# Adding the causal mask in PSUM with VectorE instead of with a bf16 matmul

## The chip, the cores and the metric

One NeuronCore of a Trainium2 chip runs the whole program in one launch. The metric is device time in microseconds (us); for the kernel before it is the median of three runs, 2414.44 us (2411.25 to 2418.63).

## What is computed

One transformer layer on x of shape (1, 2048, 512): causal attention with grouped key heads, a residual and a layer norm, then a mixture of experts (64 experts, top 8, capacity 256) with a residual and a layer norm. The change touches the attention only:

```python
# H, HKV, HD = 16, 4, 128; G = H // HKV = 4; T = 2048; q and k after RoPE
scores = jnp.einsum('bgjtd,bjsd->bgjts', q, k) * scale
mask = jnp.tril(jnp.ones((T, T), dtype=bool))
scores = jnp.where(mask[None, None, None], scores, -jnp.inf)
wei = jax.nn.softmax(scores, axis=-1)
out = jnp.einsum('bgjts,bjsd->bgjtd', wei, v)
```

## The kernel before

The program has five stages, one after the other: projections with RoPE, attention (`stage_attend`, lines 421 to 798), output projection and routing, experts, and the combination. Each stage writes out the instruction stream of every engine by hand, with semaphores between them.

The attention stage loops over the four key heads j. A head has U = 64 steps, one for each block of 128 query rows (16 of them) and each of the four query heads of the group. Step u works on query block u // 4. I count blocks from 1: block b holds the steps 4(b−1) to 4b−1, and its score rows are 128·b columns wide, because nothing to the right of the diagonal tile is computed. Up to 1024 columns (block 8) a step has one score group; from block 9 on it has two, one of 1024 columns and one with the rest. The only tile that needs a mask is the last one of a row, 128x128 on the diagonal. PSUM holds two score buffers of 1024 columns, `S[:, 0]` and `S[:, 1]`: narrow steps take them in turns, wide steps use one for each group. There are two buffers for transposes (`TP`) and two for outputs (`O`).

All matmuls on scores and values are three fp32r products of high and low parts (`split3`). In iteration i the engines do:

- TensorE (lines 583 to 664): the scores of step i (L603) and at their end the mask, a bf16 matmul of the identity with the mask tile that accumulates on the diagonal tile (L605). It waits for `exped`, with which ScalarE frees the score buffer. Then come the transposes of the probabilities of step i−3 (L615) and a half of the weighing with V for a pair of steps, five steps back (L634). Wide steps go: scores of group 0, two sets of transposes, scores of group 1, weigh, other transposes.
- VectorE (lines 712 to 784): in odd iterations the low part of an output (L760), after ScalarE's high part; then the row maximum of the first group (L732), the reciprocal of step i−1 (L743, or L745 and L748), the low parts of the first two sets of transposes (L754), the maximum of the second group and the combined maximum (L732, L736), and the low parts of the other transposes. Its queue is in this order, whatever is ready first.
- ScalarE (lines 666 to 710): in odd iterations the high part of an output (L696), high parts of transposes (L690), then exp of a group with the row sum (L681; L678 for the factor between groups), which frees the score buffer.
- GpSimd (L795) multiplies the probabilities by the reciprocal of the sum before they are transposed. SyncE loads K, V and Q and stores the outputs.

The mask tile and the identity come by DMA (`const_in`); ScalarE casts both to bf16 (L669, L670), and TensorE waits for the two casts at its start (`const_ready`, L663). The mask tile holds 0 and −1e30. The semaphore `scored` is incremented by the last matmul of a group, which is the mask matmul for the last group of a step.

Of the kernel before, what the change touches and what calls it, by code (L numbers as in the profile page):

```python
# [22 lines left out]
BF16 = mybir.dt.bfloat16  # L23
I32 = mybir.dt.int32
U32 = mybir.dt.uint32
ALU = mybir.AluOpType
# [3 lines left out]
P = 128  # L30
# [32 lines left out]
def split3(a, b):  # L63

    return ((a[LO], b[HI]), (a[HI], b[LO]), (a[HI], b[HI]))
# [355 lines left out]
def stage_attend(nc, passed, ident_d, mask_d, qk_d, v_d, o_d, wo, wo_raw, wo_in):  # L421

    U = NB * G
    blk = lambda u: u // G
    width = lambda u: (blk(u) + 1) * P
    ngrp = lambda u: 1 if width(u) <= 1024 else 2
# [12 lines left out]
    def score_group(u, a):  # L439

        return (u % 2) if ngrp(u) == 1 else a

    before, last_use = {}, {}
    for u in [u - U for u in range(U)] + list(range(U)):
        for a in range(ngrp(u % U)):
            s = score_group(u % U, a)
# [3 lines left out]
    with ExitStack() as ctx:  # L450
        def sb(name, shape, dt=F32):
            return ctx.enter_context(nc.sbuf_tensor("p2_" + name, shape, dt))

        def ps(name, shape):
            return ctx.enter_context(nc.psum_tensor("p2_" + name, shape, F32))

        def sem(name):
            return ctx.enter_context(nc.semaphore("p2_" + name))

        ident = sb("ident", [P, P])  # L460
        identb = sb("identb", [P, P], BF16)
        maskb = sb("maskb", [P, P], BF16)
        maskf = sb("maskf", [P, P])
        kT = sb("kT", [P, NT, 2, 512], F32R)
        v = sb("v", [P, NB, 2, HD], F32R)
# [13 lines left out]
        S = ps("S", [P, 2, 1024])  # L479
        TP = [ps(f"TP{k}", [P, 4, P]) for k in range(2)]  # L480
        O = [ps(f"O{k}", [P, 2, P]) for k in range(2)]

        const_in, const_ready = sem("const_in"), sem("const_ready")
        next_in, k_first, v_first, v_free = sem("next_in"), sem("k_first"), sem("v_first"), sem("v_free")
        k_in = [None] + [sem(f"k_in{c}") for c in range(1, NT)]
        v_in = [None] + [sem(f"v_in{c}") for c in range(1, NT)]
# [30 lines left out]
        def lagged(i, lag, first):  # L517

            u = i - lag
            return (u, 0) if u >= 0 else None if first else (u + U, 1)  # L520


        def steps(eng, step, tail):
            def body(j, first):
                for i in range(U):
                    step(j, i, first)
            loop(eng, HKV, body)
            for i in range(U, U + tail + 1):
                step(HKV - 1, i, False)
# [53 lines left out]
        @block.tensor  # L583
        def _(pe):
            def scores(j, u, a, first):
                b, g, tc = blk(u), u % G, u // 16
                if u == 0:
                    pe.wait_ge(k_first, j + 1)
                elif u % 16 == 0 and a == 0:
                    pe.wait_ge(k_in[tc], j * 16 + 16)  # L590
                if first and u < G - 1:
                    pe.wait_ge(q_first[u], 16)
                if a == 0 and u % 16 == (G - 1 if first and tc == 0 else 0):
                    pe.wait_ge(q_in[tc % 2], j * 32 + (16 + 16 * (tc // 2)))
                qs = [q[tc % 2][:, g, s, (b % 4) * P:(b % 4 + 1) * P] for s in (HI, LO)]
                if not (first and before[(u, a)] < 0):
                    pe.wait_ge(exped, j * SG[U] + (before[(u, a)] + 1))
                s = score_group(u, a)
                for c0 in range(a * 1024, min(width(u), a * 1024 + 1024), 512):
                    w = min(512, width(u) - c0)  # L600
                    out = S[:, s, c0 - a * 1024:c0 - a * 1024 + w]
                    for n, (x, y) in enumerate(split3(qs, [kT[:, c0 // 512, s2, 0:w] for s2 in (HI, LO)])):
                        mm = nc.tensor.matmul(out, x, y, start=(n == 0), stop=(n == 2))  # L603
                    if c0 + w == width(u):
                        mm = nc.tensor.matmul(S[:, s, width(u) - P - a * 1024:width(u) - a * 1024], identb[:],  # L605
                                              maskb[:], start=False, stop=True, skip_group_check=True)
                mm.then_inc(scored, 1)

            def turn(j, back, u, t):
                if t % 2 == 0:  # L610
                    pe.wait_ge(normed, j * SG[U] + (SG[u] + t // 2 + 1 - back * SG[U]))
                n = TG[u] + t
                pe.wait_ge(turn_lo, j * TG[U] + (n + 1 - back * TG[U]))
                for s in range(4 * t, min(4 * t + 4, blk(u) + 1)):
                    mm = nc.tensor.transpose(TP[n % 2][:, s % 4, :], prob[u % KEEP][:, s * P:(s + 1) * P], ident[:])  # L615
                mm.then_inc(turned, 1)

            def weigh(j, back, p, part, half=None):

                nb = blk(2 * p) + 1  # L620
                cut = (nb + 1) // 2
                lo, hi = ((0, cut), (cut, nb))[part]
                mid = {None: hi, 0: (lo + hi) // 2, 1: (lo + hi) // 2}[half]
                if part == 0 and half != 1:
                    if p == 0:
                        pe.wait_ge(v_first, j + 1)
                    elif p % 8 == 0:
                        pe.wait_ge(v_in[p // 8], j * 16 + 16)
                    pe.wait_ge(turn_lo, j * TG[U] + (TG[2 * p + 2] + FREE - back * TG[U]))
                    pe.wait_ge(o_lo, j * PAIRS + (p + 1 - back * PAIRS))  # L630
                for s in range(mid, hi) if half == 1 else range(lo, mid):
                    for n, (x, y) in enumerate(split3([v[:, s, h, :] for h in (HI, LO)],
                                                      [pT[p % 2][h][:, s, :, :] for h in (HI, LO)])):
                        mm = nc.tensor.matmul(O[p % 2][:], x, y, start=(s == 0 and n == 0),  # L634
                                              stop=(s == nb - 1 and n == 2))
                        if s == nb - 1 and n == 2:
                            mm.then_inc(weighed, 1)
                        elif p == PAIRS - 1 and s == cut - 1 and n == 2:
                            mm.then_inc(v_free, 1)

            def step(j, i, first):
                at = lagged(i, LAG, first)
                turns = [(j, at[1], at[0], t) for t in range(ntr(at[0]))] if at and i < U + LAG else []
                at = lagged(i, WEIGH, first)
                halves = [None]
                if len(turns) > 2 and (i >= U or ngrp(i) == 1):
                    halves = [0, 1]
                if i < U and len(halves) == 1:
                    scores(j, i, 0, first)
                if len(halves) == 2:  # L650
                    weigh(j, at[1], at[0] // 2, at[0] % 2, 0)
                for args in turns[0:2]:
                    turn(*args)
                if i < U and len(halves) == 2:
                    scores(j, i, 0, first)
                if i < U and ngrp(i) == 2:
                    scores(j, i, 1, first)
                if at and i < U + WEIGH:
                    weigh(j, at[1], at[0] // 2, at[0] % 2, halves[-1])
                for args in turns[2:]:  # L660
                    turn(*args)

            pe.wait_ge(const_ready, 2)  # L663
            steps(pe, step, WEIGH - 1)

        @block.scalar
        def _(act):
            act.wait_ge(const_in, 32)
            nc.scalar.copy(identb[:], ident[:]).then_inc(const_ready, 1)  # L669
            nc.scalar.copy(maskb[:], maskf[:]).then_inc(const_ready, 1)  # L670
            act.sem_inc(weighed, FREE)

            def exp(j, u, a):
# [37 lines left out]

        @block.vector
        def _(dve):
            dve.sem_inc(turn_lo, FREE)
            dve.sem_inc(o_lo, FREE)

# [10 lines left out]
            def row_max(j, u, a):  # L727
                k, wide = u % KEEP, ngrp(u) == 2
                dve.wait_ge(scored, j * SG[U] + (SG[u] + a + 1))
                w = min(1024, width(u) - a * 1024)  # L730
                out = (nmax if a == 0 else nmax1) if wide else nm
                r = nc.vector.reduce_max(out[:, k:k + 1], S[:, score_group(u, a), 0:w], AX_X, negate=True)  # L732
                r.then_inc(max_part if a == 1 else max_ready, 1)
                if a == 1:
                    dve.wait_ge(max_part, j * (SG[U] - U) + (SG[u + 1] - u - 1))
                    nc.vector.tensor_tensor(nm[:, k:k + 1], nmax[:, k:k + 1], nmax1[:, k:k + 1], ALU.min  # L736
                                            ).then_inc(max_ready, 1)
# [958 lines left out]
```

## Time and profile before

| | |
|---|---|
| Median of three runs | 2414.44 us (2411.25 to 2418.63) |
| Profiled execution, first to last instruction | 2450.7 us |
| Difference of the profiled span to the median | 36.3 us, 1.5% |
| Attention stage in it | about 328 to 1395 us |
| Mean granted clock of TensorE | 0.934 of full speed |
| TensorE busy / weight loads / VectorE / ScalarE / GpSimd | 2104.8 / 1802.7 / 1749.9 / 1371.8 / 1125.8 us |

Of the profiled execution only the span is given, with no separate time around it; all durations below are from this one execution. TensorE is called PE in the rows, its weight loads PEld, VectorE DVE, ScalarE ACT and GpSimd POOL. Matmuls are pipelined, and a matmul's duration is its latency: what it costs a stream is read from the distance of starts. Where an engine's idle time is shown, the name behind the arrow is what ended it.

### The profile page before, as it was taken

The numbers are of one execution on the slowest core, as the hardware profiler recorded it, in microseconds if no ns is written. First come the engines' busy times: TensorE is split into PE (matmuls) and PEld (weight loads), VectorE is DVE, ScalarE is ACT, GpSimd is POOL, SyncE is SP. The second block draws the span as 40 slices with busy tenths as digits, with TensorE's granted clock in tenths as the row PEclk, the third lists the DMA queues.
The fourth block names the chain that finished last, engine by engine and source line by source line (L and its number), as shares of the span: only waits on it lengthen the run. The fifth ranks groups of instructions, "written<-read, shape, count | busy, mean of one in ns | idle before, by whom it ended". The sixth has DMA issues, their size and how long they took to land. (4 is left out here: it accounts for less than half of the span.)

```text
span 2450.7 us, 43821 instructions
## 1 busy us (share of the span) xinstructions
PE 2104.8 (86%) x13313; PEld 1802.7 (74%) x13313; DVE 1749.9 (71%) x3146; ACT 1371.8 (56%) x2755; POOL 1125.8 (46%) x1093
## 2 busy tenths in 40 slices
PE   8999969999999999999999989982999999996000
PEld 6777758988899888988899877772888888884000
DVE  5899967876787677776787645553777777774657
ACT  3899946665676567665676532222566666663000
POOL 1455523332333223332333226664666666664675
PEclk9999979999999999999999999995999999997555
DMA  7444462012411051104300065432788888884775
GB/s 241 176 193 193 188 250 88 27 57 86 135 62 57 24 190 70 57 22 162 121 35 23 23 237 174 174 128 97 255 263 278 263 265 273 265 268 160 216 235 182
DMA packets 145296, 380.61 MB, mean 155 GB/s; under 512 B 19584, under 2 KB 37120, under 8 KB 140544
## 3 DMA queue, kind: packets, MB, share of 16 engines
q1 hardware_dynamic: 120576, 311.61, 37.1%
q0 software_dynamic: 24576, 67.20, 8.3%
q8 instruction: 75, 1.23, 0.2%
q14 instruction: 69, 0.57, 0.1%
HBM read 252.78 MB, written 125.96 MB: 155 GB/s over the span
## 5 line engine op out<-in xcount | busy, mean ns | idle before, releaser
L603 PE MATMUL p_S<-p_kT,p_q 128*128 128x512 f32 (+3 forms) x1920 | 475.0, 377 | 31.8 <-DMA p_q<-qk_scratch 25.1
L603 PEld LDWEIGHTS p_S<-p_kT,p_q 128*128 128x128 f32 x1920 | 324.7, 190 | 81.0 <-issue 27.3
L795 POOL TENSOR_SCALAR p_prob<-p_prob,p_inv,p_part 128x1024 f32<-128x1024 f32 x128 | 153.0, 1196 | 496.1 <-DVE p_inv L748 496.1
L615 PE MATMUL p_TP<-p_ident,p_prob 128*128 128x128 f32 x2176 | 303.5, 274 | 1.8 <-DVE p_pT1l L754 1.8
L795 POOL TENSOR_SCALAR p_prob<-p_prob,p_inv 128x128 f32<-128x128 f32 (+7 forms) x256 | 191.5, 748 | 241.4 <-DVE p_inv L743 241.4
L732 DVE TENSOR_REDUCE p_nmax<-p_S 128x1 f32<-128x1024 f32 (+7 forms) x256 | 251.7, 983 | 23.1 <-PE p_S L603 22.1
L615 PEld LDWEIGHTS p_TP<-p_ident,p_prob 128*128 128x128 f32 x2176 | 245.5, 141 | 25.9 <-DVE p_pT1l L754 5.6
L690 ACT CAST p_pT1h<-p_TP 128x512 fp32r<-128x512 f32 (+3 forms) x320 | 154.8, 526 | 153.5 <-PE p_TP L615 153.3
L690 ACT CAST p_pT0h<-p_TP 128x512 fp32r<-128x512 f32 (+3 forms) x320 | 155.1, 527 | 150.4 <-PE p_TP L615 149.2
L634 PE MATMUL p_O<-p_pT0h,p_v 128*128 128x256 f32 x1088 | 227.6, 293 | 6.0 <-DVE p_pT0l L754 6.0
L634 PE MATMUL p_O<-p_pT1h,p_v 128*128 128x256 f32 x1088 | 226.0, 292 | 5.6 <-issue 3.2
L754 DVE TENSOR_TENSOR p_pT1l<-p_TP,p_pT1h 128x512 fp32r<-128x512 f32 (+3 forms) x320 | 182.3, 603 | 60.2 <-ACT p_pT1h L690 59.4
L754 DVE TENSOR_TENSOR p_pT0l<-p_TP,p_pT0h 128x512 fp32r<-128x512 f32 (+3 forms) x320 | 182.2, 603 | 50.1 <-ACT p_pT0h L690 49.1
L681 ACT ACTIVATE p_prob<-p_S,p_nm 128x128 f32<-128x128 f32 (+7 forms) x256 | 189.6, 741 | 28.7 <-DVE p_nm L732 27.3
L416 POOL TENSOR_TENSOR p_qr<-p_rc,p_rs 128x512 f32<-128x512 f32 x80 | 131.4, 1643 | 120.6 <-DVE p_rs L365 120.6
L634 PEld LDWEIGHTS p_O<-p_pT0h,p_v 128*128 128x128 f32 x1088 | 178.7, 191 | 7.0 <-issue 5.1
L634 PEld LDWEIGHTS p_O<-p_pT1h,p_v 128*128 128x128 f32 x1088 | 178.0, 191 | 7.0 <-issue 3.6
L916 PE MATMUL p_acc<-p_woh,p_ot 128*128 128x512 f32 x512 | 174.6, 413 | 8.4 <-DMA p_ot<-o_scratch 8.4
L1104 POOL DMA_INDIRECT slot_scratch<-p_tok,p_slot_i x128 | 127.0, 992 | 93.3 <-DVE p_slot_i L1065 55.5
L1550 POOL DMA_INDIRECT p_rows<-y_scratch,p_idx x128 | 135.2, 1056 | 65.1 <-issue 35.9
L1466 POOL DMA_INDIRECT p_xg<-x_scratch,p_idx x128 | 129.3, 1010 | 73.3 <-POOL p_idx L1462 52.0
L681 ACT ACTIVATE p_prob<-p_S,p_nmax 128x1024 f32<-128x1024 f32 x128 | 144.2, 1127 | 24.2 <-DVE p_nmax L732 22.8
(212 smaller groups left out, 5061.0 us busy)
## 6 DMA issues: line engine op xcount, KB each, us to landing
p_w_raw<-in_gu SPq DMA_DIRECT2D x64, 768.0 KB
qk_scratch<-p_qout SPq DMA_DIRECT2D x80, 512.0 KB, 2.6
o_scratch<-p_oT SPq DMA_DIRECT2D x128, 256.0 KB, 2.1
p_ot<-o_scratch SPq DMA_DIRECT2D x32, 1024.0 KB
y_scratch<-p_y SPq DMA_DIRECT2D x128, 256.0 KB
p_q<-qk_scratch SPq DMA_DIRECT2D x15, 2048.0 KB, 9.2
p_w_raw<-in_gu SPq DMA_DIRECT2D x64, 256.0 KB
v_scratch<-p_vout SPq DMA_DIRECT2D x16, 512.0 KB, 3.2
```

Source lines behind the costliest of these rows:

```text
L416: nc.gpsimd.tensor_tensor(qr[t][:], rc[t % 2][:], rs[t % 2][:], ALU.add).then_inc(q_rot, 1)
L603: mm = nc.tensor.matmul(out, x, y, start=(n == 0), stop=(n == 2))
L615: mm = nc.tensor.transpose(TP[n % 2][:, s % 4, :], prob[u % KEEP][:, s * P:(s + 1) * P], ident[:])
L634: mm = nc.tensor.matmul(O[p % 2][:], x, y, start=(s == 0 and n == 0), stop=(s == nb - 1 and n == 2))
L681: nc.scalar.activation(prob[k][:, a * 1024:a * 1024 + w], S[:, score_group(u, a), 0:w], ACT.Exp, bias=top[:, k:k + 1], accum_out=rsum[:, k ...
L690: nc.scalar.copy(pT[p % 2][HI][:, 4 * t:4 * t + m, u % 2, :], TP[n % 2][:, 0:m, :]).then_inc(turn_hi, 1)
L732: r = nc.vector.reduce_max(out[:, k:k + 1], S[:, score_group(u, a), 0:w], AX_X, negate=True)
L754: nc.vector.tensor_tensor(pT[p % 2][LO][:, 4 * t:4 * t + m, u % 2, :], TP[n % 2][:, 0:m, :], pT[p % 2][HI][:, 4 * t:4 * t + m, u % 2, :].b ...
L795: nc.gpsimd.tensor_scalar(prob[k][:, cols], prob[k][:, cols], inv[:, k:k + 1], scale, ALU.mult, ALU.mult).then_inc(normed, 1)
L916: mm = nc.tensor.matmul(acc[k][:], a, w, start=(n == 0 and m == 0), stop=(n == H - 1 and m == 2))
L1466: nc.gpsimd.indirect_dma_start(out=xg[k][c][:], out_offset=None, in_=x1_d, in_offset=bass.IndirectOffsetOnAxis(ap=idx[k][:, c:c + 1], axis ...
L1550: nc.gpsimd.indirect_dma_start(out=rows[k][n][:], out_offset=None, in_=y_d, in_offset=bass.IndirectOffsetOnAxis(ap=idx[k][:, n:n + 1], axi ...
```

## The change

The mask matmul, the two bf16 tiles and the casts go. TensorE waits for the DMA of the constants instead of for the casts. In the last score group of every step VectorE adds the fp32 mask tile to the diagonal tile in PSUM, waits for its own addition, and then takes the row maximum. `scored` is now incremented by the last matmul of the scores.

```diff
@@ stage_attend @@
-        identb = sb("identb", [P, P], BF16)
-        maskb = sb("maskb", [P, P], BF16)
...
-        const_in, const_ready = sem("const_in"), sem("const_ready")
+        const_in, covered = sem("const_in"), sem("covered")
...
                         mm = nc.tensor.matmul(out, x, y, start=(n == 0), stop=(n == 2))
-                    if c0 + w == width(u):
-                        mm = nc.tensor.matmul(S[:, s, width(u) - P - a * 1024:width(u) - a * 1024], identb[:],
-                                              maskb[:], start=False, stop=True, skip_group_check=True)
                 mm.then_inc(scored, 1)
...
-            pe.wait_ge(const_ready, 2)
+            pe.wait_ge(const_in, 32)
             steps(pe, step, WEIGH - 1)
 
         @block.scalar
         def _(act):
-            act.wait_ge(const_in, 32)
-            nc.scalar.copy(identb[:], ident[:]).then_inc(const_ready, 1)
-            nc.scalar.copy(maskb[:], maskf[:]).then_inc(const_ready, 1)
             act.sem_inc(weighed, FREE)
...
         @block.vector
         def _(dve):
+            dve.wait_ge(const_in, 32)
             dve.sem_inc(turn_lo, FREE)
...
                 out = (nmax if a == 0 else nmax1) if wide else nm
+                if a == ngrp(u) - 1:
+                    last = S[:, score_group(u, a), w - P:w]
+                    nc.vector.tensor_tensor(last, last, maskf[:], ALU.add).then_inc(covered, 1)
+                    dve.wait_ge(covered, j * U + u + 1)
                 r = nc.vector.reduce_max(out[:, k:k + 1], S[:, score_group(u, a), 0:w], AX_X, negate=True)
```

## Rows read from the trace of the kernel before

**Rows 1.** The page's head and its line of busy times

```profile
span 2450.7 us, 43821 instructions
...
PE 2104.8 (86%) x13313; PEld 1802.7 (74%) x13313; DVE 1749.9 (71%) x3146; ACT 1371.8 (56%) x2755; POOL 1125.8 (46%) x1093
```

**Rows 2.** Busy time by stretch, third head: blocks 1-2, 3-4, 6-10, 11-16

```profile
core 0: us, PE busy (x) PEld busy (x) DVE busy (x) ACT busy (x) POOL busy (x), PEclk, DMA share, GB/s
851.50:877.70 26.20, 23.44 (x194) 22.04 (x192) 13.98 (x39) 11.68 (x34) 4.75 (x9) 1.00 0.39 137
877.70:890.30 12.60, 12.19 (x86) 9.95 (x85) 10.37 (x30) 10.24 (x30) 5.29 (x9) 1.00 0.67 214
898.90:971.20 72.30, 71.95 (x515) 64.67 (x514) 56.29 (x119) 50.26 (x119) 24.14 (x27) 1.00 0.32 111
971.20:1121.70 150.50, 147.91 (x1052) 133.16 (x1051) 113.63 (x219) 98.56 (x219) 47.99 (x48) 1.00 0.10 36
```

**Rows 3.** Groups by line and shape: busy us, mean ns, idle before

```profile
L605 PE MATMUL p_S<-p_maskb,p_identb 128*128 128x128 bf16 x256 | 59.6, 233 | 0.0
...
L754 DVE TENSOR_TENSOR p_pT1l<-p_TP,p_pT1h 128x128 fp32r<-128x128 f32 x32 | 9.0, 280 | 0.0
```

**Rows 4.** Timeline of TensorE: mask ahead of transposes, mask ahead of a weigh (start, us)

```profile
928.20 0.23 PE L605 MATMUL p_S<-p_maskb,p_identb 128*128 128x128 bf16 x1
928.26 0.61 PE L615 MATMUL p_TP<-p_ident,p_prob 128*128 128x128 f32 x4
...
1340.17 0.23 PE L605 MATMUL p_S<-p_maskb,p_identb 128*128 128x128 bf16 x1
...
1340.41 0.28 PE L634 MATMUL p_O<-p_pT0l,p_v 128*128 128x256 f32 x1
1340.53 0.28 PE L634 MATMUL p_O<-p_pT0h,p_v 128*128 128x256 f32 x1
```

**Rows 5.** Timeline of ScalarE: its first exp of the stage

```profile
329.82 0.37 ACT L681 ACTIVATE p_prob<-p_S,p_nm 128x128 f32<-128x128 f32 x1 [8.57 <-DVE p_nm L732]
```

**Rows 6.** Timeline, two steps of block 4 (u = 13, 14, then 15)

```profile
885.45 0.68 DVE L732 TENSOR_REDUCE p_nm<-p_S 128x1 f32<-128x512 f32 x1
...
886.58 0.68 DVE L732 TENSOR_REDUCE p_nm<-p_S 128x1 f32<-128x512 f32 x1
...
887.97 0.36 ACT L696 CAST p_oT<-p_O 128x256 fp32r<-128x256 f32 x1
888.37 0.42 DVE L760 TENSOR_TENSOR p_oT<-p_O,p_oT 128x256 fp32r<-128x256 f32 x1 [0.40 <-ACT p_oT L696]
...
888.71 0.68 DVE L732 TENSOR_REDUCE p_nm<-p_S 128x1 f32<-128x512 f32 x1
```

**Rows 7.** Timeline of VectorE: row maxima of even steps, blocks 5, 6 and 7

```profile
890.28 0.82 DVE L732 TENSOR_REDUCE p_nm<-p_S 128x1 f32<-128x640 f32 x1 [0.24 <-PE p_S L605]
...
898.93 0.96 DVE L732 TENSOR_REDUCE p_nm<-p_S 128x1 f32<-128x768 f32 x1 [0.43 <-PE p_S L605]
...
904.06 0.96 DVE L732 TENSOR_REDUCE p_nm<-p_S 128x1 f32<-128x768 f32 x1 [0.60 <-PE p_S L605]
...
915.16 1.09 DVE L732 TENSOR_REDUCE p_nm<-p_S 128x1 f32<-128x896 f32 x1 [0.69 <-PE p_S L605]
```

**Rows 8.** Timeline, from block 9's last step (u = 35) to block 10

```profile
948.49 0.42 DVE L760 TENSOR_TENSOR p_oT<-p_O,p_oT 128x256 fp32r<-128x256 f32 x1 [0.97 <-ACT p_oT L696]
948.83 1.21 DVE L732 TENSOR_REDUCE p_nmax<-p_S 128x1 f32<-128x1024 f32 x1
...
951.10 0.19 ACT L681 ACTIVATION_READ_ACCUMULATOR p_prob<-p_S,p_nmax 128x1 f32 x1
...
951.34 1.68 PE L603 MATMUL p_S<-p_kT,p_q 128*128 128x512 f32 x6
```

**Rows 9.** Timeline of block 16 (u = 61, then the scores of 62)

```profile
1099.47 1.22 DVE L732 TENSOR_REDUCE p_nmax<-p_S 128x1 f32<-128x1024 f32 x1
...
1100.72 0.16 DVE L736 TENSOR_TENSOR p_nm<-p_nmax 128x1 f32<-128x1 f32 x1
...
1102.19 0.30 ACT L678 ACTIVATE p_part<-p_nmax,p_nm 128x1 f32<-128x1 f32 x1
...
1103.64 1.66 PE L603 MATMUL p_S<-p_kT,p_q 128*128 128x512 f32 x6
```

## The prediction

> **What bounds the kernel now.** I read the head and the busy line of the page first [rows 1]: TensorE is busy for 86% of the span and VectorE for 71%. Such shares average stages with different limits, so the second view is the busy time in stretches of the attention stage. The stage does the same work for each of four key heads; I use the third, from 850.8 to 1121.7 us [rows 2]. A head has 64 steps (u = 0 to 63); four steps make a block, and in block b the score rows are 128·b columns wide. The reader is to see two regimes. From 898.9 us on (block 6) TensorE has almost no gap (71.95 of 72.30, 147.91 of 150.50) and VectorE is busy for 78 and 76%. In blocks 3 and 4, 877.7 to 890.3, VectorE and ScalarE are each at 82 and 81%, and TensorE, at 97%, hides short waits behind its modelled ends. The granted clock is 1.00 in all of them. So the change trades time on an engine that is the limit in the wide blocks for time on one that is nearly the limit in the narrow ones, and the question is where each amount counts. The answer is the same in each head, so what a block gives counts 16 times (4 steps, 4 heads).
>
> **Removed: 256 mask matmuls on TensorE.** The group shows x256 at 233 ns [rows 3], but that is latency. What one takes from the stream is read from starts [rows 4]. Ahead of a weigh, from the mask matmul's start to the start of the second weigh matmul pass 1340.41 − 1340.17 = 0.24 us, where two weigh matmuls are otherwise 0.12 apart (1340.41 to 1340.53): 0.24 − 0.12 = **0.12 us**. That is the case of the 32 wide steps of a head (blocks 9 to 16). Ahead of transposes, as in nearly all narrow steps, the first starts 0.06 after the mask matmul and four take (0.61 − 0.27)/3 = 0.11 each, which is their usual pitch: **0.07 us**. If TensorE were the limit everywhere this were 128 × 0.12 + 128 × 0.07 = 24 us.
> The Trainium skill (TensorE: Matmul & The Clock Gate, section Back-to-back issue gap) gives about 81 ns for one weight load and matmul of 128 columns in a stream. By that figure 256 would be worth 21 us, and the wide steps 0.08 instead of 0.12 each; the trace's larger number is used.
>
> **Removed: two casts on ScalarE** ahead of the stage. Nothing: ScalarE waits 8.57 us after them for the first row maximum [rows 5]. If that wait were gone they would be worth at most 0.7 us (two 128x128 instructions, each no longer than the 0.37 of the exp in that row).
>
> **Added: 256 VectorE additions of a 128x128 tile in PSUM, and a wait of VectorE on its own result.** No row shows VectorE writing PSUM. The nearest is the 128x128 subtraction that reads PSUM, 280 ns [rows 3]. Bounds: a 128x1 instruction takes 0.16 [rows 9], the 128x256 subtraction from PSUM 0.42 [rows 8]. I take 0.28. The dependent instruction after a VectorE result starts 0.03 later (a maximum ends at 1099.47 + 1.22 = 1100.69, the next starts at 1100.72 [rows 9]). So **0.31 us** a step, 0.19 to 0.45 by the bounds. Queued behind it on VectorE are the row maximum, the reciprocal that releases GpSimd, and the low parts that release the transposes' PSUM; behind the maximum ScalarE's exp, which frees the score buffer.
> The Trainium skill (VectorE: DVE Perf Modes, section Rules for kernel authors) says that chained VectorE instructions each pay the pipeline and that the op count is to be kept small. It speaks against this change; its formula for an fp32 two-tensor op would give 0.29 for 128 elements, an estimate from that page, which would leave the sum as it is within 1 us.
>
> **Where the 0.31 counts, block by block.**
> Blocks 3 and 4. The limit is a round trip over two steps [rows 6]: maximum of the odd step at 885.45, maximum of the even step at 886.58, then its exp on ScalarE, then the output cast on ScalarE (887.97), for which VectorE idles 0.40, the low part of the output (888.37), and the next odd maximum at 888.71. These 3.26 us are VectorE and ScalarE one after the other, and TensorE is not in them. Both additions of the two steps lie in it; the idle time of 0.40 is no room, since what it waits for is behind the even addition. +0.31 a step; TensorE's saving is worth nothing.
> Blocks 5 to 8. The same round trip, but the even maximum now waits for TensorE [rows 7]: 0.24 in the first pair of block 5 and nothing that the view prints in the second (I take 0.19 for both), 0.43 and 0.60 in block 6, 0.69 in block 7 and more in block 8. Independent VectorE instructions overlap by 0.08 (888.37 + 0.42 against 888.71 [rows 6]), so the room is the wait plus 0.08. Block 5: (0.62 − 0.27)/2 = +0.18 a step. Block 6: (0.62 − 0.60)/2 = +0.01. Blocks 7 and 8: room for both, TensorE sets the pace, −0.07.
> Blocks 9 and 10. The mask lies in the second of two score groups, but the round trip over two steps passes through it once: low part of the output (948.49), odd first maximum (948.83, behind it), exp, whose buffer TensorE waits for (scores again at 951.34) [rows 8], even maximum, and then the even second group with its addition. In this pair nothing is free: the scores follow the exp at once. Wider groups leave some room, so I allow 0.1 as a mean of the two blocks: (0.31 − 0.10)/2 = +0.11 a step; TensorE's saving is lost here too. Block 11 lies between this and the next case, 0.
> Blocks 12 to 16. The addition is hidden: in block 16 the combined maximum is there at 1100.88, and ScalarE, behind the high parts of the last transposes, takes it at 1102.19 [rows 9]. If that cover of 1.3 us were gone, each would cost 0.31. The time to 1103.64, where TensorE reuses the buffer, runs through the weigh and the transposes after the mask, so the saving counts whole: −0.12 a step.
> Blocks 1 and 2. VectorE is busy for 14 of 26.9 us [rows 2], mostly waiting for the end of the head before. The first step and the last already wait for VectorE, the others gain 0.07: +1 us in all, −2 to +10 by the same prices in none or in all 32 steps.
>
> **The sum.** Per step 0.31 + 0.31 + 0.18 + 0.01 − 0.07 − 0.07 + 0.11 + 0.11 + 0 − 5 × 0.12 = +0.29; times 16 is 4.6, with blocks 1 and 2 **+5.6 us**. The profiled execution spans 2450.7 us, so it would span 2456.3. It was 36 us (1.5%) longer than the median of the runs, 2414.4; I put the difference on the median: **2420 us**. With 0.19 for the addition the blocks give −0.35 a step, −5.6 us; with 0.45 it reaches block 7 and 11, +1.21 a step, 19.4 and 2 more. So this case goes from 2409 to 2436, most of it 2412 to 2429. A measurement of this kernel tells about 0.3% (7 us) from no change.
>
> **Rivals.**
> *The VectorE round trip binds further than block 6.* Slower. Mechanism: PSUM writes cost VectorE more than reads, or the low parts, which come 0.62 late in even steps, hold the transposes. It decides once the two additions exceed the room of 0.69 + 0.08 = 0.77 in block 7, that is at 0.39 each. Then blocks 3 to 7 pay 0.31 or more (80 × 0.31 = 25), blocks 9 to 11 0.16 (8), and blocks 8 and 12 to 16 give back 11: +22 us, **2436**. For: no row shows such a write, and in block 6 the room is just used up. Against: the nearest rows are 0.28 and TensorE has almost no gap in the stretch from 898.9 [rows 2]. 0.22.
> *Part of the addition is hidden.* Faster. Mechanism: the 0.40 idle ahead of the output's low part takes one of two additions, and the free parts of blocks 9 to 11 are larger. Blocks 3 and 4 then give +0.16, 5 to 7 −0.07, 8 the same, 9 to 11 −0.12: 0.32 − 0.28 − 0.36 − 0.60 = −0.92 a step, −15 us, **2400**. Against it: ScalarE's cast starts right behind the even exp in [rows 6]. 0.17.
> *TensorE's clock falls.* TensorE waits for longer in blocks 3 and 4 with fewer matmuls. At 1.2 GHz their 12.19 us of matmuls would take up to 24; some of it fills the waits, so I take +9 us a head over my forecast, **2456**. Against: the clock stayed at 1.00 (2.4 GHz) through blocks 1 and 2, where TensorE has 2.8 us of gaps [rows 2]. 0.03. The Trainium skill (TensorE: Matmul & The Clock Gate, section Why this matters for your kernels) warns of clock drops after idle gaps; no gap of this stage brought one on.
> *It doesn't do what it says:* the mask matmuls were hidden under weight loads, and nothing comes back. The 0.24 in [rows 4] speaks against it. Without the 0.12 and 0.07 of blocks 7, 8 and 12 to 16 the sum is +17 us, 2431: inside the first rival's reach and counted there.
>
> **Chances.** My forecast 0.58: 0.38 within 0.3%, 0.20 above it. Round trip 0.22 and clock 0.03, all slower. Hidden 0.17: 0.13 faster, 0.04 within. Faster 0.13, same 0.42, slower 0.45. Range 2403 to 2437: it takes in the bounds of the addition and most of the faster case; forecast and slower cases hold most of the chance on one side.
>
> **What would show it.** In the changed profile: additions of 0.26 to 0.32 us; step pairs of blocks 3 and 4 longer by 0.6 us (3.26 to 3.9); blocks 12 to 15 shorter by 0.12 a step with TensorE still without gaps; weigh matmuls at 0.12 right behind the scores; blocks 7 and 8 slightly shorter. I am wrong if the addition takes over 0.4, if blocks 3 and 4 hardly grow, if blocks 12 to 16 don't shrink, or if the time moves outside the attention stage.

## The result, and the profile after

The changed kernel takes 2419.61 us (median of six runs, 2416.75 to 2424.07), the kernel before 2414.27 us (six runs on the same chip). The ratio of the runs is 1.0026, with a 95% interval of 1.0014 to 1.0038: slower by 0.26%, inside what I had called hard to tell from no change, and 0.4 us beside the predicted 2420. In microseconds the ratio says +6.3 (3.4 to 9.2), the two medians alone +5.3. Differences of timed runs below are worked out from the ratio.

The span of the changed kernel's profiled execution can't be set against the 2450.7 us of [rows 1]. To judge by the stages behind the attention (last section), the kernel before was profiled on a slower chip, of the kind on which it takes 2450 us (below). The attention stage can be compared, because nearly all steps of its last three heads repeat to about 0.02 us, from head to head and from chip to chip, but for single stretches that are named below. The stage runs to 1409 us in the profile of before, where its last weigh matmul starts, and not to the 1395 that I had given for its end. The page's head and busy line of the changed kernel:

```profile
span 2418.7 us, 43755 instructions
...
PE 2089.3 (86%) x13057; PEld 1801.1 (74%) x13057; DVE 1827.6 (76%) x3402; ACT 1376.3 (57%) x2753; POOL 1130.2 (47%) x1093
```

TensorE has 256 matmuls and 15.5 us of busy time less, VectorE 256 instructions and 77.7 us more. Now the busy time in stretches of the third head, first the kernel before, then the changed one. The stretches go from the first score matmul of a block to that of another: blocks 3 and 4, blocks 9 and 10, blocks 12 to 15. (They start 0.7 to 1.7 us earlier than those of [rows 2], which went by row maxima.)

```profile
core 0: us, PE busy (x) PEld busy (x) DVE busy (x) ACT busy (x) POOL busy (x), PEclk, DMA share, GB/s
876.89:889.03 12.14, 11.73 (x83) 9.39 (x82) 10.15 (x30) 9.88 (x29) 4.68 (x8) 1.00 0.66 206
...
933.88:969.49 35.61, 35.26 (x252) 31.74 (x250) 27.68 (x62) 25.15 (x63) 11.95 (x15) 1.00 0.26 90
988.88:1086.89 98.01, 98.01 (x697) 88.25 (x696) 75.23 (x146) 64.18 (x145) 32.52 (x33) 1.00 0.12 44
```

```profile
881.80:896.73 14.93, 12.29 (x75) 9.96 (x74) 12.17 (x38) 9.62 (x30) 4.69 (x8) 1.00 0.57 173
...
941.71:978.20 36.49, 35.50 (x244) 31.25 (x242) 29.61 (x70) 25.57 (x63) 12.42 (x15) 1.00 0.24 87
997.42:1093.62 96.20, 96.20 (x682) 87.99 (x680) 79.77 (x163) 64.46 (x145) 32.86 (x34) 1.00 0.12 45
```

The reader is to see three outcomes of one change. The narrow blocks 3 and 4 grow from 12.14 to 14.93 us, 0.35 a step. Blocks 9 and 10 grow from 35.61 to 36.49, 0.11 a step. Blocks 12 to 15 shrink from 98.01 to 96.20, 0.11 a step, with TensorE without a gap before and after, and VectorE going from 77 to 83% at no cost. The granted clock is 1.00 in all six.

Measured in this way for all four heads, from the first score matmul of each block to the next, the attention stage is 9.4 us longer. Of this 2.6 us is a slower TensorE clock, in two stretches of 3.4 us. The first is at the start of the second head, whose first step takes 8.82 us against 7.26 in the third. The second is at that head's end, whose last step takes 13.38 us against 12.30 in the third. In both the granted clock is at half (1.2 GHz). Here the stretches, and the weigh matmuls of the second head's first step beside those of the third's, which come 0.12 apart where the slow ones come 0.22 apart:

```profile
585.18:587.90 2.72, 2.71 (x13) 2.72 (x14) 0.20 (x1) 0.00 (x0) 0.00 (x0) 0.51 0.54 139
...
851.48:854.89 3.41, 3.41 (x16) 3.41 (x17) 0.69 (x1) 0.28 (x1) 0.00 (x0) 0.50 0.03 10
```

```profile
585.18 0.55 PE L629 MATMUL p_O<-p_pT0h,p_v 128*128 128x256 f32 x1 [1.48 <-DVE p_pT0l L751]
585.53 0.42 PE L629 MATMUL p_O<-p_pT0l,p_v 128*128 128x256 f32 x1
585.75 0.63 PE L629 MATMUL p_O<-p_pT0h,p_v 128*128 128x256 f32 x2
...
859.92 0.38 PE L629 MATMUL p_O<-p_pT0h,p_v 128*128 128x256 f32 x1 [1.48 <-DVE p_pT0l L751]
860.13 0.28 PE L629 MATMUL p_O<-p_pT0l,p_v 128*128 128x256 f32 x1
860.25 0.40 PE L629 MATMUL p_O<-p_pT0h,p_v 128*128 128x256 f32 x2
```

Ahead of each TensorE had idled, for 1.48 and 2.20 us; but the third head has the same 1.48 and stays at full clock, and so do all changes of heads of the kernel before. The rest, 6.7 us, lies inside the interval of the timed runs.

The addition in the groups by line (busy us, mean ns of one, idle before and what ended it):

```profile
L727 DVE TENSOR_TENSOR p_S<-p_S,p_maskf 128x128 f32<-128x128 f32 x256 | 74.5, 291 | 26.5 <-PE p_S L601 25.7
```

It takes 0.29 us, just over the 0.28 of its nearest row in [rows 3]. The timeline of block 4 in the changed kernel, steps u = 12 to 14, which answers to [rows 6]:

```profile
890.66 0.69 DVE L729 TENSOR_REDUCE p_nm<-p_S 128x1 f32<-128x512 f32 x1
...
892.06 0.36 ACT L688 CAST p_oT<-p_O 128x256 fp32r<-128x256 f32 x1
...
892.46 0.42 DVE L757 TENSOR_TENSOR p_oT<-p_O,p_oT 128x256 fp32r<-128x256 f32 x1 [0.58 <-ACT p_oT L688]
892.80 0.29 DVE L727 TENSOR_TENSOR p_S<-p_S,p_maskf 128x128 f32<-128x128 f32 x1
893.12 0.69 DVE L729 TENSOR_REDUCE p_nm<-p_S 128x1 f32<-128x512 f32 x1
...
894.25 0.29 DVE L727 TENSOR_TENSOR p_S<-p_S,p_maskf 128x128 f32<-128x128 f32 x1
...
894.58 0.69 DVE L729 TENSOR_REDUCE p_nm<-p_S 128x1 f32<-128x512 f32 x1
```

Two steps now take 894.58 − 890.66 = 3.92 us where they took 3.26. The difference, 0.66, is twice 0.33: an addition of 0.29 and a gap of 0.03 to 0.04 in front of the dependent maximum (892.80 + 0.29 = 893.09 to 893.12; 894.25 + 0.29 = 894.54 to 894.58). And the place where the matmul stood, TensorE going from scores to a weigh, to be read beside [rows 4]:

```profile
1005.54 0.28 PE L629 MATMUL p_O<-p_pT0h,p_v 128*128 128x256 f32 x1
1005.66 0.27 PE L629 MATMUL p_O<-p_pT0l,p_v 128*128 128x256 f32 x1
1005.77 0.40 PE L629 MATMUL p_O<-p_pT0h,p_v 128*128 128x256 f32 x2
```

The weigh matmuls come at 0.12 from the first one on; there is no distance of 0.20 to 0.24 any more.

### The profile page after: what moved, and what is told of

Its sections match the earlier page's. It is cut to its first block and busy times, and to the rows that moved or that the text cites. A ratio compares the mean times of both kernels' runs of the same rounds, so it can differ in the third digit from the quotient of the medians.

```text
span 2418.7 us, 43755 instructions
## 1 busy us (share of the span) xinstructions
PE 2089.3 (86%) x13057; PEld 1801.1 (74%) x13057; DVE 1827.6 (76%) x3402; ACT 1376.3 (57%) x2753; POOL 1130.2 (47%) x1093
## 5 line engine op out<-in xcount | busy, mean ns | idle before, releaser
L610 PEld LDWEIGHTS p_TP<-p_ident,p_prob 128*128 128x128 f32 x2176 | 250.6, 141 | 41.1 <-DVE p_pT0l L751 9.5
L629 PEld LDWEIGHTS p_O<-p_pT0h,p_v 128*128 128x128 f32 x1088 | 178.6, 191 | 10.4 <-issue 7.4
```

## The experiments

The question was where each part counts: the matmul alone, the addition alone, and the addition in odd and in even steps. The first four kernels ran on one chip and the last four on another, each next to the kernel before, which takes 2450.39 us on the first and 2451.22 on the second; ratios are to that. For each run the blocks were measured in its one profile. A short table first; its numbers are microseconds a step, as the change against the kernel before, a mean over the 16 steps of a block in four heads (last two rows: us in all). They are worked out from the starts of the score matmuls. Behind the stage's first 10 us, which are at half clock in every profile, the clock fell to half for 3.4 us in four of the ten profiles: twice in the changed kernel and twice with both, once in the even steps and once with the addition ahead of the wait. These are the four with an addition in the even steps of blocks 1 to 4; with one profile of each, that the additions bring the drops on isn't shown. The drops are in the table. They add 2.6 us to the stage of the changed kernel, 2.1 with both and 1.5 in the even steps, so the three are +6.7, about +21.8 and +1.5 without them.

| block | predicted | changed | neither | both | odd | even |
|---|---|---|---|---|---|---|
| 3 | +0.31 | +0.33 | −0.01 | +0.34 | +0.14 | +0.14 |
| 4 | +0.31 | +0.34 | +0.06 | +0.34 | +0.17 | +0.19 |
| 5 | +0.18 | +0.05 | −0.06 | +0.06 | −0.03 | −0.03 |
| 6 | +0.01 | +0.14 | −0.07 | +0.17 | 0.00 | −0.01 |
| 7 | −0.07 | −0.06 | −0.08 | 0.00 | −0.04 | −0.04 |
| 8 | −0.07 | −0.08 | −0.08 | 0.00 | −0.04 | −0.04 |
| 9 | +0.11 | +0.11 | 0.00 | +0.11 | 0.00 | +0.05 |
| 10 | +0.11 | +0.08 | −0.05 | +0.08 | −0.05 | +0.08 |
| 11 | 0 | −0.05 | −0.11 | +0.01 | −0.05 | −0.02 |
| 12 to 16, mean | −0.12 | −0.10 | −0.12 | +0.01 | −0.06 | −0.06 |
| 1 and 2, us | +1 | +4.0 | −1.5 | +5.3 | +1.7 | +2.5 |
| stage, us | +5.6 | +9.4 | −17.3 | +23.9 | −1.5 | +3.0 |

**Neither matmul nor addition.** The changed kernel without the addition and its wait:

```diff
-        const_in, covered = sem("const_in"), sem("covered")
+        const_in = sem("const_in")
...
-                if a == ngrp(u) - 1:
-                    last = S[:, score_group(u, a), w - P:w]
-                    nc.vector.tensor_tensor(last, last, maskf[:], ALU.add).then_inc(covered, 1)
-                    dve.wait_ge(covered, j * U + u + 1)
```

> Neither matmul nor addition: the diagonal tile is left unmasked, so the softmax takes in keys to the right of the diagonal inside the tile. Theory (TensorE is the limit from block 5 on except in 9 and 10, a VectorE and ScalarE round trip in 3, 4, 9, 10): blocks 3 and 4 stay at 1.35 and 1.69 us a step, blocks 12 to 16 shrink by 0.12 as in the changed kernel, 5 to 8 by 0.07; -14 to -18 us against before, about 2398. Rival A (the mask matmul was hidden under weight loads, and blocks 12 to 16 shrank for another reason): all blocks as before, 2414. Rival B (the matmul counts in every step): blocks 3 and 4 shrink by 0.07 too, -24 us, 2390.

2434.46 us, ratio 0.994 (0.9921 to 0.9958), −14.7 us (−19 to −10). This kernel leaves the mask out. Blocks 3 and 4, then 12 to 15 of the third head:

```profile
866.24:878.90 12.66, 11.60 (x76) 9.93 (x74) 10.07 (x30) 9.68 (x29) 4.68 (x8) 1.00 0.62 195
976.96:1073.14 96.18, 96.18 (x682) 88.03 (x680) 75.40 (x146) 64.22 (x145) 32.70 (x34) 1.00 0.12 45
```

Blocks 12 to 15 take 96.18 us, as in the changed kernel (96.20): the whole of the matmul's time comes back there, and the addition costs nothing. So rival A falls. Blocks 3 and 4 don't gain (12.66 here; in the first and last head they are within 0.05 a step of before, and in the two middle ones the first step of block 4 has an extra of 0.40 and 0.48 us that I can't place). So rival B falls too. The saving, 14.7 us in the timing and 17.3 in the stage, is what the theory said, and the 24 of the matmul counted everywhere lie outside the interval.

**Both.** The kernel before with the addition in every step and the matmul kept. This version and all that follow but the one with the addition ahead of the wait are edits of the kernel before, with the two casts still in place; `on_dve` says which steps VectorE masks, `on_pe` which TensorE masks:

```diff
+    on_dve = lambda u: True
+    on_pe = lambda u: True
...
-                    if c0 + w == width(u):
+                    if c0 + w == width(u) and on_pe(u):
...
+                if a == ngrp(u) - 1 and on_dve(u):
+                    last = S[:, score_group(u, a), w - P:w]
+                    nc.vector.tensor_tensor(last, last, maskf[:], ALU.add).then_inc(covered, 1)
+                    dve.wait_ge(covered, j * ND[U] + (ND[u] + 1))
```

> Matmul and addition both, so the tile gets the mask twice. Theory: the addition alone shows. Blocks 3 and 4 longer by 0.31 to 0.35 a step, 9 and 10 by 0.12 or a little more, 7, 8 and 12 to 16 within 0.03 of before since the addition is hidden there; +20 to +24 us, about 2436. Rival (the addition also costs a little in the wide blocks, and the saving of the matmul was larger than 0.12): blocks 12 to 16 longer by 0.05 to 0.3 a step, +28 us or more, above 2442.

2473.93 us, ratio 1.0094 (1.0069 to 1.0119), +23 us. The same two stretches:

```profile
888.32:903.28 14.96, 12.71 (x84) 9.54 (x82) 12.21 (x38) 9.63 (x30) 4.68 (x8) 1.00 0.54 172
1004.95:1102.92 97.97, 97.97 (x698) 88.26 (x696) 79.71 (x163) 64.28 (x145) 32.50 (x33) 1.00 0.12 44
```

14.96 beside 14.93: in blocks 3 and 4 it makes no difference whether the matmul is there. 97.97 beside 98.01: in blocks 12 to 15 it makes no difference whether the addition is there. The rival's extra in the wide blocks isn't there. The two parts lie on different limits. Added up, −14.7 and +23 give +8, within the interval of the change itself.

**Odd steps, even steps.** The addition in every other step and the matmul in the rest:

```diff
+    on_dve = lambda u: u % 2 == 1
+    on_pe = lambda u: not on_dve(u)
```

The other run has `u % 2 == 0`.

> Addition in odd steps, matmul in even ones. Theory: in blocks 9 and 10 the round trip over two steps passes the second score group of the even step only, so they stay at 4.36 and 4.54 us a step; blocks 3 and 4 longer by 0.16 to 0.18; 12 to 16 shorter by 0.06. About +2 us. Rival (each addition costs VectorE time that counts wherever it stands): blocks 9 and 10 longer by 0.06 each, here and in the even version alike.

> Addition in even steps, matmul in odd ones. Theory: blocks 9 and 10 as in the changed kernel (4.50 and 4.63 us a step), since the even addition lies in the round trip; blocks 3 and 4 longer by 0.16 to 0.18; 12 to 16 shorter by 0.06. About +4 us. Rival: blocks 9 and 10 longer by 0.06 each, as in the odd version.

One run each: 2450.67 and 2451.64 us, which the timing doesn't tell from before; what follows is from the profiles. The stage is at −1.5 us where +2 was expected, and at +1.5 without its clock drop where +4 was. Blocks 9 and 10, the stretch of some 36 us in the third head, odd first, then even:

```profile
933.74:969.14 35.40, 34.97 (x247) 31.47 (x246) 28.48 (x66) 25.33 (x63) 12.18 (x15) 1.00 0.26 90
```

```profile
936.15:972.29 36.14, 35.63 (x247) 31.57 (x246) 28.59 (x66) 25.18 (x63) 12.00 (x15) 1.00 0.25 88
```

With four additions in odd steps the stretch is 35.40, shorter than before (35.61) and as long as without matmul and addition (35.42 in that run): these four additions cost nothing. With four in even steps it is 36.14, 0.7 us longer. The two runs differ in the place of the matmuls too, but all eight matmuls of the stretch are worth only the 0.2 between 35.61 and 35.42, so 0.5 us or more is the place of the additions in the round trip, and the rival (VectorE time counts wherever it stands) falls. In block 10 the even run gives 4.62 us a step as the theory said (4.63), the odd one 4.49 where 4.54 was expected, because a matmul there is worth a little after all. In block 9 the even steps alone give +0.05, half of the +0.11 with all additions, and the odd ones alone nothing, so the odd ones take part once the even ones are there. In block 6 each half costs nothing and both together 0.14 to 0.17.

**The addition ahead of the wait.** In odd narrow steps VectorE adds the mask ahead of the output's low part, where it idles for ScalarE:

```diff
+            early = lambda u: ngrp(u) == 1 and u % 2 == OUT % 2
...
+                if i < U and early(i):
+                    cover(j, i)
                 if at and i % 2 == OUT % 2:
                     out_lo(j, at[1], at[0] // 2)
```

`cover` waits for the scores of the step and adds the mask tile; in all other steps it is called where the addition stood.

> The changed kernel, with the addition of odd narrow steps put ahead of the output's low part on VectorE, where it idles 0.40 us waiting for ScalarE. Theory (round trip over two steps): that addition leaves the round trip, and blocks 3 and 4 are longer than before by 0.16 to 0.18 a step instead of 0.34; block 5 and 6 back at or under before. Rival (VectorE is simply full there, its time counts wherever it stands): blocks 3 and 4 stay at 1.71 and 2.02 a step.

2448.33 us in one run. Timeline of VectorE in block 4, steps 12 to 14:

```profile
884.38 0.69 DVE L737 TENSOR_REDUCE p_nm<-p_S 128x1 f32<-128x512 f32 x1
...
885.51 0.29 DVE L726 TENSOR_TENSOR p_S<-p_S,p_maskf 128x128 f32<-128x128 f32 x1
...
886.18 0.42 DVE L765 TENSOR_TENSOR p_oT<-p_O,p_oT 128x256 fp32r<-128x256 f32 x1 [0.38 <-ACT p_oT L688]
886.52 0.68 DVE L737 TENSOR_REDUCE p_nm<-p_S 128x1 f32<-128x512 f32 x1
...
887.64 0.29 DVE L726 TENSOR_TENSOR p_S<-p_S,p_maskf 128x128 f32<-128x128 f32 x1
887.97 0.69 DVE L737 TENSOR_REDUCE p_nm<-p_S 128x1 f32<-128x512 f32 x1
```

Two steps take 887.97 − 884.38 = 3.59 us: one addition (0.33) less than the 3.92 above, with the same work on VectorE. It stands in the idle time before the low part, and 0.38 of that is left. In the second and third heads blocks 3 and 4 are longer than before by 0.16 and 0.17 a step, as expected, and the rival falls. Block 6 is back at 2.56 to 2.61 us a step (2.59 before). The run also shows a wait that the runs so far didn't. In the fourth head the first step of block 3 takes 3.06 us beside 1.46 to 1.53 in the other heads:

```profile
1147.51 0.37 ACT L688 CAST p_oT<-p_O 128x256 fp32r<-128x256 f32 x1 [1.49 <-DMA o_scratch<-p_oT]
```

ScalarE waits for the store of an output. The queue of the stores also issues, once, the load of 12 of the 16 row blocks of Wo (3 MB), at the start of the fourth head. In this run, and in the two below with the changed order, the load is issued 9.0 to 9.3 us into the head and is still under way when the next store is issued, and that store takes 10.0 to 10.4 us to land. In the seven other profiles it is issued at 5.5 to 6.0 us and has landed by then, and the store takes 6.6 to 7.6 us. So the Wo load that comes late seems to hold the store up; moving it wasn't tried. A clock drop of 3.4 us follows this wait.

**A split of the mask, and a change of order.** The runs point to a version: the addition where it was free, the matmul elsewhere; and, apart from it, VectorE taking the row maximum of odd steps ahead of the output's low part, since that wait is in the round trip of blocks 3, 4, 9 and 10.

```diff
+    on_dve = lambda u: (u // 4 + 1 in (7, 8)) or (u // 4 + 1 >= 11) or (u // 4 + 1 in (5, 9, 10) and u % 2 == 1)
...
+                if i < U:
+                    row_max(j, i, 0)
                 if at and i % 2 == OUT % 2:
                     out_lo(j, at[1], at[0] // 2)
...
-                if i < U:
-                    row_max(j, i, 0)
                 if former and i < U + 1:
```

> VectorE adds the mask where that was free so far: all steps of blocks 7, 8 and 11 to 16, odd steps of 5, 9 and 10; the matmul masks the rest (blocks 1 to 4, 6, even steps of 5, 9, 10). Theory: each block moves as it did in the run where that choice was made: 5 by -0.03 a step, 6 by 0, 7 and 8 by -0.07, 9 by 0, 10 by -0.05, 11 by -0.05 to -0.1, 12 to 16 by -0.13, -0.08, -0.12, -0.13, -0.13; times 16 -12 to -14 us, ratio 0.994 to 0.995, better than both kernels. Rival (VectorE's extra time in the wide blocks comes back at the change of heads or elsewhere): less than half of it, -6 us or less.

> The kernel before with one change of order: in odd steps VectorE takes the first group's row maximum ahead of the output's low part. The mask stays on TensorE. Theory: the maximum of 0.55 to 0.68 leaves the round trip; block 3 falls by about 0.1 a step, block 4 by 0.03 until TensorE limits it, 9 and 10 by 0.05 each; -3 to -5 us. Rival: the output's low part, now later, holds the weigh or the stores, and nothing is won or blocks get longer.

> The mask split of the version with additions in chosen steps, and the order of the version with the maximum first. Theory: both gains add, -15 to -19 us, ratio about 0.993. Rival: the order takes back room that the additions use, and it is no better than the split alone.

The split alone: 2435.87 us, ratio 0.995 (0.9934 to 0.9966), −12 us (−16 to −8); in its profile the stage is 12.7 us shorter, block by block as expected but for block 6 (+0.04 a step). The rival, that VectorE's time comes back elsewhere, falls. The order alone: 2447.58 us, 0.9986 (0.9970 to 1.0002), −3.4 us, which the timing doesn't tell from nothing; in the profile block 3 takes 1.22 us a step in three heads instead of 1.35, block 4 1.67 instead of 1.69, block 9 4.34 instead of 4.36 and block 10 stays (0.05 less was expected in both), and in the fourth head the first step of block 3 has the wait for the store again (2.81 us), so that the stage gains only 0.7. Here the rival, which had the low part hold the stores, was half right. Both: 2433.39 us, ratio **0.9932 (0.9909 to 0.9954)**, −16.7 us, better than both kernels (the changed one stands at 1.0026 to the kernel before on its chip). In the fourth head the wait for the store is there too (2.32 us). Its three stretches of the third head, blocks 3 and 4, 9 and 10, 12 to 15:

```profile
868.28:879.90 11.62, 11.44 (x84) 9.28 (x83) 10.46 (x30) 9.55 (x30) 4.68 (x8) 1.00 0.74 212
924.05:959.28 35.23, 34.80 (x248) 31.40 (x246) 28.84 (x66) 25.04 (x63) 12.58 (x15) 1.00 0.27 95
978.21:1074.38 96.17, 96.17 (x681) 87.98 (x680) 79.80 (x163) 63.47 (x145) 32.59 (x34) 1.00 0.12 45
```

Each is at or under the better of the two kernels: 11.62 beside 12.14 and 14.93, 35.23 beside 35.61 and 36.49, 96.17 beside 98.01 and 96.20. Most of the gain is the split; the intervals don't tell it from the split alone; the one profile of each has 16.4 against 12.7 us in the stage.

## Why the prediction was right, and where not

**Price of the matmul.** Ahead of a weigh I had 0.12 us a step; blocks 12 to 16 gave 0.12 as a mean without matmul and addition, 0.12 to 0.13 in blocks 12 and 14 to 16, but 0.08 in block 13, where the last scores are 128 columns wide. Ahead of transposes I had 0.07; blocks 7 and 8 gave 0.08. The Trainium skill's 81 ns (TensorE: Matmul & The Clock Gate, section Back-to-back issue gap) fits the narrow blocks and is a third too low for the wide ones: here the row was the better price.

**Price of the addition.** I had 0.31 with the wait; 3.92 − 3.26 gives 0.33 each. The formula of the Trainium skill for an fp32 addition of two tensors (VectorE: DVE Perf Modes, section The TRN2 errata), which the page checked at 512 and 2048 elements, gives an estimate of 0.29 for 128, and the group's mean of 291 ns agrees, with PSUM as source and destination. The skill's rule to keep the number of VectorE instructions small (same page, section Rules for kernel authors) holds in blocks 3 and 4 and not in 12 to 15, where the same instruction in each step cost nothing (97.97 beside 98.01 us).

**The round trip of blocks 3 and 4.** Right in place and size: +0.31 predicted, +0.33 and +0.34. That the matmul is worth nothing there is shown by the run without either, that the idle 0.40 doesn't take up the additions by the changed kernel, and that it can, once the order is changed, by the run with the addition first. The rival in which part is hidden named the right idle time, but VectorE's order kept the addition out of it, and its gain in blocks 9 to 11 didn't come.

**Blocks 5 and 6.** Off in both, and the two errors cancel: +0.18 and +0.01 predicted, +0.05 and +0.14 measured, together 0.19 both times. The room of block 5 was larger than the waits of the even maxima let me think. In block 6 a mean of four steps hides what happened: in each of the last three heads its first step is 0.73 us longer, and the other three are 0.05 to 0.08 shorter, as in blocks 7 and 8. So the step of the prediction that failed is "the room is the wait plus 0.08", pair by pair. VectorE falls behind through block 5 at little cost, and at the first step of block 6 TensorE waits for a low part. The waits of the stage, before and after (us, times, longest):

```profile
ACT p_prob L681 <- DVE p_nm L732: 27.3, 39, 8.6
...
PEld p_TP L615 <- DVE p_pT0l L754: 4.1, 16, 0.3
```

```profile
ACT p_prob L673 <- DVE p_nm L729: 79.8, 116, 15.9
...
PEld p_TP L610 <- DVE p_pT0l L751: 9.5, 25, 0.8
```

and in the first step of block 6, where there was none before:

```profile
907.30 0.76 PE L610 MATMUL p_TP<-p_ident,p_prob 128*128 128x128 f32 x5 [0.59 <-DVE p_pT0l L751]
```

The low part that it waits for stands on VectorE behind the additions of two steps. It is the second mechanism of my first rival (low parts 0.62 late hold the transposes), at one step and not in five blocks. That it needs both additions fits: with one of them, in either place, block 6 costs nothing.

**Blocks 9 and 10.** +0.11 and +0.11 predicted, +0.11 and +0.08 measured, and the odd and even runs show that the even addition is the one in the round trip, in block 10 alone, in block 9 for about half. But in block 9 the right mean is luck. Its first three steps are as long as before, within 0.02 us, and the last one (u = 35, from its scores to those of block 10) is 0.54 longer in three heads and 0.22 in the first. First before, then changed:

```profile
946.88 1.66 PE L603 MATMUL p_S<-p_kT,p_q 128*128 128x512 f32 x6
...
951.34 1.68 PE L603 MATMUL p_S<-p_kT,p_q 128*128 128x512 f32 x6
```

```profile
954.70 1.66 PE L601 MATMUL p_S<-p_kT,p_q 128*128 128x512 f32 x6
...
959.69 1.65 PE L601 MATMUL p_S<-p_kT,p_q 128*128 128x512 f32 x6
```

4.46 us become 4.99. This is the very step of [rows 8]: I had read the round trip where it binds and taken it for the whole block. In block 10 it does bind pair by pair, at 0.20 and 0.13 us a pair (0.21 predicted).

**Blocks 11 and 12 to 16:** 0 and −0.12 predicted, −0.05 and −0.10 measured. Block 16 gave less (−0.07) only because the second clock drop stands at the end of the second head; without its 1.1 us block 16 is at −0.14 and the mean at −0.12.

**Blocks 1 and 2.** The weakest term: +1 us predicted, +4.0 measured, of which 1.6 is the first clock drop. Of the other 2.4 most is in the first three steps of a head, 0.2 to 0.27 us each, and in the third step of block 2, 0.4 us; I had allowed for the first and the last step alone.

**The sum.** The forecast of +5.6 us came out at 6.7 in the stage without the clock drops, 9.4 with them, and 5.3 (medians) or 6.3 (ratio) in the timing. The closeness of 2420 to 2419.6 is partly luck: blocks 5, 6, and 1 and 2 are off by 1.4 to 2.1 us each, and the 2420 rests on taking 36 us off the span of the profile. That was right, but the 36 us are for the most part the slower chip of that profile (last section), which the working didn't know. Two slips in the working changed nothing: the lower bound of the addition gives about −0.28 a step by the prices shown and not −0.35, and the range from 2403 leaves out the 2400 of the faster rival.

**The rivals.** The addition took 0.29 and not over 0.39, so block 7 kept its gain and the slow case didn't come. The clock did fall, for 3.4 us at two places, at the start and at the end of a head and not in blocks 3 and 4 as the rival had it, and it cost 2.6 us in the profile and not 36. That no gap of this stage brings a drop on was true of the kernel before and isn't of the changed one. "It doesn't do what it says" falls with the run without either.

## What to carry to other kernels

An operation that moves from one engine to another has no one worth: read it for each width of the loop, from which engine has no gaps there and from whether the receiving instruction stands in a round trip or in an idle stretch. Where the two kernels win in different blocks, a choice made step by step at build time can beat both, as it did here; and where an in-order engine idles in front of one instruction, ask which ready work could stand ahead of it before taking work away from it. And compare two profiles step by step before believing a mean: here two blocks had a plausible mean and all of its cost in one step, and a slower clock looked like a wait until the distances of the matmuls were read.

## What had not been expected of the hardware

The kernel before takes 2414 us on the chip of the first comparison and 2450 and 2451 on the two chips of the experiments, 1.5% apart, where the runs on one chip lie within about 0.7% of each other. To judge by the profiles, the difference lies behind the attention stage. From the start of its last weigh matmul (1409.3 us) the profile of before has 1041 us to go, the one with odd additions (1407.2) 1042, and the changed kernel on its chip 1001. Of these 40 us 26 lie in the stretch up to the long run of expert matmuls and 14 behind it, while that run takes 522.2 us in both. What makes those stretches slower wasn't looked into. It is why only ratios within a chip stand in this text, and why the blocks of the attention stage could be compared across all of them.
